# A two-layer graph kernel on one core: three products with both weight halves side by side, the first normalisation on ScalarE, and head and tail in orders of their own

## Chip, cores and metric

One Trainium2 chip, one of its cores. The metric is the device time in microseconds of one execution of the whole program; the data lie in HBM at the start and the result goes back there.

## What is computed

Eight graphs (B = 8) of N = 1024 nodes with D = 128 features, each with a dense 1024 x 1024 adjacency of zeros and ones. All data are float32.

```python
v, q, k = relu(x @ Wv + bv), relu(x @ Wq + bq), relu(x @ Wk + bk)
att = softmax(scores * adj - 9e15 * (1 - adj))        # scores = q @ k.T
x = layernorm(x + relu(att @ v @ Wo + bo))
h = x @ W_w.T + W_b
u = adj * exp(e[:, :, None] + f[:, None, :] + a_b)    # e = h @ a1, f = h @ a2
out = layernorm(x + (u / u.sum(axis=2, keepdims=True)) @ h)
```

## The kernel before

Nodes are taken in T = 8 tiles of 128. Nearly every matrix operand is split in two fp32r parts, a rounded one ("hi", here `h`) and what is left ("lo", here `l`), and a product of two matrices is three matmuls (hi x hi, lo x hi, hi x lo) that are summed in PSUM (`product`, L824 to L826). So each operand costs a rounding, mostly on ScalarE (ACT), and a subtraction, on VectorE (DVE, out of PSUM) or GpSimd (POOL, in SBUF).

For one batch: `project_q` and `project_k` make q and k transposed, in halves of 512 nodes; `project_v` makes v in halves of four tiles. ACT evicts q and k with bias and relu, DVE evicts v (`v_out`, L568). For each of 8 tiles `scores` fills the two banks of `s_ps`; DVE adds the penalty of the absent edges and finds the row extreme (`mask_max`, L578); ACT takes the exponential (`probs`); PE transposes it in two halves (`transpose_p`, into `pt_ps`), ACT and DVE split it (`prob_hi`, `prob_lo`). `attend` multiplies two tiles with v at a time (into `av_ps`), again split by `av_hi` and `av_lo`. `project_out` multiplies with Wo, in two halves; DVE scales by the row sum and adds the bias in place in PSUM (`o_out`, L596 to L601), adds x (`residual0`, L608), takes statistics (`stats0`), POOL the power -1/2, DVE normalises (`norm0`, L630). For the second layer `transpose_x1`, `x1_hi`, `x1_lo`, then `project_h` (130 columns: h and the two logit parts), `exp_ef`, and g = h times an exponential, split out of PSUM by `g_hi` (ACT, L446) and `g_lo` (DVE, L642). `aggregate` multiplies a tile of the rounded transposed adjacency (`round_adj`, ACT, L370, from two staging slots into a ring of four) with all of g, 8 matmuls of 258 columns; DVE adds the two parts (`agg_out`, L655). Then the row scale (`scale_out`), the residual (`residual1`, POOL), statistics, power and second normalisation (`norm1`, POOL) and the store. POOL also turns each adjacency tile into a penalty (`convert`, L256) and makes the lower parts of x, q, k and v.

Order: every engine, and SP with its queue of transfers, has one list of steps written by hand (`batch_pass`), run for all passes with the parts of absent batches left out; three batches are in flight. What PE puts in PSUM outside the scores, transposes and `attend` goes round three banks `m_ps` in the order of the table `SLOTS`, 22 uses a pass; PE waits in `shared` until the use three places before has been evicted. `transpose_p` waits for `prob_lo` of the tile before, `scores` for `mask_max` of the tile before, `k_hi` of a batch for the last scores of the batch before. The head is the same list with most parts absent: x first, q before k, lower parts on POOL. The tail is the same list too: the last batch's eight aggregations come after all the rest, each behind its `round_adj`, and then `scale_out`, `residual1` in halves, `stats1`, the power, `norm1` and two stores.

Of the kernel before, what the change touches and what calls it, by code (L numbers as in the profile page):

```python
# [5 lines left out]
F32 = mybir.dt.float32  # L6
# [6 lines left out]
EPS = 1e-5  # L13
# [4 lines left out]
def resnorm_kernel(nc, x, x_t, adj, adj_t_tiles, pack_a, pack_b, out):  # L18
# [11 lines left out]
    WARM = 13  # L30
    assert D == P and T == 8

    with ExitStack() as ctx:
# [13 lines left out]
        w_h, w_l = sb("w_h", [P, 4, D], F32R), sb("w_l", [P, 4, D], F32R)  # L47
# [26 lines left out]
        ef = sb("ef", [P, T, 2])  # L74
        g = sb("g", [P, T, 2, G1], F32R)
# [8 lines left out]
        var0, var1, rstd0, rstd1 = (sb(n, [P, T]) for n in ("var0", "var1", "rstd0", "rstd1"))  # L84
# [34 lines left out]
        out_free = [sem(f"out_free{k}") for k in range(2)]  # L119
        passed = sem("passed")  # L120
# [38 lines left out]
        SLOTS = (  # L159
# [4 lines left out]
        )  # L164
        PASSES = range(-1, B + 2)
        filled, bank, before = [], {}, {}
        for p in PASSES:
            for what, part, behind in SLOTS:
                if there(p - behind):
                    use = (what, p - behind, part)  # L170
                    bank[use] = m_ps[len(filled) % BANKS]
                    before[use] = filled[-BANKS] if len(filled) >= BANKS else None
                    filled.append(use)

        emptied = {"q": (q_evac, 2), "k": (k_evac, 2), "v": (v_evac, 2), "o": (y_done, 2), "x1t": (x1tl_done, 2),
                   "h": (gl_done, TH), "agg": (agg_done, T)}
# [5 lines left out]
        def _(sp):  # L182
# [900 lines left out]
```

## Time and profile before

| | us |
|---|---|
| runs (3): lowest, median, highest | 435.87, 435.93, 440.18 |
| the profiled execution, whole | 435.52 |
| its span in the trace | 433.8 |
| PE busy | 405.0 |
| DVE busy | 325.8 |
| ACT busy | 307.1 |
| POOL busy | 260.9 |

The span reaches from the first to the last recorded event; what lies around it, 1.7 us, is start and end of the program. The granted clock of PE has a mean of 0.976 of full speed. The engines: PE is TensorE (PEld its loading of weights), DVE is VectorE, ACT ScalarE, POOL GpSimd, SP the engine that issues transfers. L and a number is a line of the kernel. Busy intervals of PE overlap the next one's start, so the distance from one start to the next tells what a matmul takes in a sequence.

### The profile page before, as it was taken

The page shows a single profiled execution, that of the slowest core. Times are in us where ns is not written, and L with a number is a line of the kernel's source. Part 1 is how long each engine was busy: PE and PEld are TensorE (multiplying, and loading weights), DVE is VectorE, ACT ScalarE, POOL GpSimd, SP SyncE. Part 2 cuts the span into 40 slices and gives each one's busy share as a digit, 9 for nine tenths or more (in the row PEclk, how much of TensorE's full clock was granted, in tenths as well). Part 3 has the DMA queues.
Part 4 walks back from the last instruction along what each step waited for, and adds up shares of the span by engine and source line. Part 5 has one row for each costly group of instructions (what it writes and reads, how often), then busy time and mean ns, then how long its engine had stood idle before and what let it go on. Part 6 is the DMA issues. An engine that isn't in the chain of part 4 may idle for free.

```text
span 433.8 us, 8721 instructions
## 1 busy us (share of the span) xinstructions
PE 405.0 (93%) x2944; PEld 377.6 (87%) x2944; DVE 325.8 (75%) x929; ACT 307.1 (71%) x569; POOL 260.9 (60%) x223
## 2 busy tenths in 40 slices
PE   8699999999999999999999999999999999997730
PEld 7589999999999999999999999999999999996630
DVE  2566689587887888797887878787887979878631
ACT  4586779787878778696878778696878677765510
POOL 3943753474266972779356972779357852752955
PEclk9999999999999999999999999999999999999685
DMA  6763355465472739385474738385464737247431
GB/s 225 247 249 100 97 195 210 179 202 187 163 275 85 261 113 335 97 278 194 153 286 115 275 107 328 108 280 201 138 251 107 269 116 254 81 146 219 171 97 48
DMA packets 36684, 80.72 MB, mean 186 GB/s; under 512 B 2592, under 2 KB 19104, under 8 KB 36640
## 3 DMA queue, kind: packets, MB, share of 16 engines
q1 hardware_dynamic: 36352, 79.70, 54.4%
q8 instruction: 24, 0.39, 0.3%
q10 hardware_dynamic: 288, 0.46, 0.3%
q14 instruction: 20, 0.16, 0.1%
HBM read 75.96 MB, written 4.19 MB: 185 GB/s over the span
## 4 chain that ended last, share of the span: by engine, by line
PE 85%; POOL 5%; DVE 4%; DMA 3%; ACT 2%; issue 1%; POOLq 0%; DVEq 0%; ACTq 0%
PE pt_ps L877 12%; PE m_ps L928 12%; PE av_ps L889 7%; PE av_ps L890 7%; PE av_ps L891 7%; PE s_ps L824 7%; PE s_ps L826 7%; PE s_ps L825 6%; PE m_ps L826 6%; PE m_ps L825 6%; PE m_ps L824 6%; DMA adjt_in<-in_adj_t_dram 2%; PE m_ps L906 2%; DMA xt_in<-in_x_t_dram 1%; DVE prob L578 1%
## 5 line engine op out<-in xcount | busy, mean ns | idle before, releaser
L586 DVE TENSOR_TENSOR prob_tl<-pt_ps,prob_th 128x512 fp32r<-128x512 f32 x128 | 84.5, 682 | 24.5 <-ACT prob_th L417 24.4
L578 DVE CUSTOM_DVE_ANT_0 prob<-s_ps,penalty 128x1024 f32<-128x1024 f32 x64 | 78.0, 1219 | 23.4 <-PE s_ps L826 21.5
L417 ACT ACTIVATE prob_th<-pt_ps 128x512 fp32r<-128x512 f32 x128 | 73.1, 593 | 28.4 <-PE pt_ps L877 28.3
L370 ACT ACTIVATE adj_t<-adjt_in 128x1024 fp32r<-128x1024 f32 x64 | 67.1, 1056 | 24.7 <-PE m_ps L928 13.8
L409 ACT ACTIVATE prob<-prob,neg_max 128x1024 f32<-128x1024 f32 x64 | 73.8, 1152 | 12.5 <-DVE neg_max L578 12.4
L928 PE MATMUL m_ps<-g,adj_t 128*128 128x258 f32 x512 | 76.2, 295 | 4.9 <-DVE g L649 1.9
L877 PE MATMUL pt_ps<-ident,prob 128*128 128x128 f32 x512 | 73.7, 273 | 0.0
L889 PE MATMUL av_ps<-prob_th,vh 128*128 128x256 f32 x256 | 73.6, 287 | 0.0
L928 PEld LDWEIGHTS m_ps<-g,adj_t 128*128 128x128 f32 x512 | 67.2, 195 | 6.4 <-ACT adj_t L370 2.7
L891 PE MATMUL av_ps<-prob_th,vl 128*128 128x256 f32 x256 | 72.4, 283 | 0.0
L890 PE MATMUL av_ps<-prob_tl,vh 128*128 128x256 f32 x256 | 72.3, 283 | 0.0
L256 POOL TENSOR_SCALAR penalty<-adj_in 128x1024 bf16<-128x1024 f32 x64 | 66.4, 1051 | 5.9 <-issue 5.9
L877 PEld LDWEIGHTS pt_ps<-ident,prob 128*128 128x128 f32 x512 | 59.2, 140 | 5.4
L824 PE MATMUL s_ps<-kh,qh 128*128 128x512 f32 x128 | 53.2, 416 | 3.8 <-DVE neg_max L578 2.2
L265 POOL TENSOR_TENSOR ql<-qf,qh 128x512 fp32r<-128x512 f32 x16 | 20.6, 1286 | 55.7 <-ACT qh L388 55.6
L826 PE MATMUL s_ps<-kh,ql 128*128 128x512 f32 x128 | 50.3, 393 | 0.0
L825 PE MATMUL s_ps<-kl,qh 128*128 128x512 f32 x128 | 50.2, 392 | 0.0
L889 PEld LDWEIGHTS av_ps<-prob_th,vh 128*128 128x128 f32 x256 | 49.0, 191 | 0.3 <-issue 0.2
L890 PEld LDWEIGHTS av_ps<-prob_tl,vh 128*128 128x128 f32 x256 | 49.0, 191 | 0.1
L891 PEld LDWEIGHTS av_ps<-prob_th,vl 128*128 128x128 f32 x256 | 49.0, 191 | 0.0
L655 DVE TENSOR_REDUCE gs<-m_ps 128x129 f32<-128x258 f32 x64 | 25.9, 419 | 19.0 <-POOL out_sb L303 10.0
L269 POOL TENSOR_TENSOR kl<-kf,kh 128x512 fp32r<-128x512 f32 x16 | 20.6, 1287 | 20.3 <-ACT kh L400 20.3
(101 smaller groups left out, 881.4 us busy)
## 6 DMA issues: line engine op xcount, KB each, us to landing
adj_in<-in_adj_dram SPq DMA_DIRECT2D x64, 512.0 KB, 4.3
adjt_in<-in_adj_t_dram SPq DMA_DIRECT2D x64, 512.0 KB, 4.3
xt_in<-in_x_t_dram SPq DMA_DIRECT2D x8, 512.0 KB, 6.6
x_in<-in_x_dram SPq DMA_DIRECT2D x8, 512.0 KB, 4.7
out_dram<-out_sb SPq DMA_DIRECT2D x16, 256.0 KB, 4.4
wb<-in_pack_b_dram ACTq DMA_DIRECT2D x1, 320.0 KB, 6.3
wa<-in_pack_a_dram ACTq DMA_DIRECT2D x1, 132.0 KB, 4.4
```

The lines of the kernel that those rows point to most:

```text
L409: sc.activation(prob[i % 2][:, :], prob[i % 2][:, :], ACT.Exp, bias=neg_max[:, i:i + 1], scale=-1.0, accum_out=row_sum[b % 2][:, i:i + 1]) ...
L417: sc.activation(prob_th[n % 2][:, tiles(k), (i % 2) * P:(i % 2 + 1) * P], pt_ps[k][:, :].rearrange("p (c n) -> p c n", n=P), ACT.Copy).the ...
L578: v.tensor_tensor_reduce(out=prob[i % 2][:, :], in0=s_ps[:, :, :].rearrange("p a n -> p (a n)"), in1=penalty[:, n % RING, :], scale=-1.0, ...
L586: v.tensor_tensor(prob_tl[n % 2][at], pt_ps[k][:, :].rearrange("p (c n) -> p c n", n=P), prob_th[n % 2][at].bitcast(F32), ALU.subtract).th ...
L824: pe.matmul(dst, lh, rh, start=True, stop=False)
L825: pe.matmul(dst, lh, rl, start=False, stop=False)
L826: return pe.matmul(dst, ll, rh, start=False, stop=True)
L877: last = pe.transpose(blk(pt_ps[k], c), blk(prob[i % 2], k * TH + c), ident[:, :])
L889: pe.matmul(av_ps[:, 0:PAIR], vh[:, c, :], th[:, c, :], start=(c == 0), stop=False)
L890: pe.matmul(av_ps[:, 0:PAIR], vh[:, c, :], tl[:, c, :], start=False, stop=False)
L891: last = pe.matmul(av_ps[:, 0:PAIR], vl[:, c, :], th[:, c, :], start=False, stop=(c == T - 1))
L928: last = pe.matmul(a[:, 0:2 * G1], adj_t[:, n % RING, c, :], g[:, c, :, :].rearrange("p a e -> p (a e)"), start=(c == 0), stop=(c == T - 1))
```

## The change

Three products, v, output projection and h, are now made with the high and low weight halves in one moving operand (`w_hl`, `w1hl`): the first matmul has 256 (260) columns and leaves hi x hi and hi x lo beside each other in PSUM, the second adds lo x hi to the first half. The eviction adds the two. v and the output projection now go through a bank two tiles at a time (four parts a batch), h one tile at a time (eight parts).

```diff
+            def product_side_by_side(dst, lhs, rhs, width):
+                lh, ll = lhs
+                pe.matmul(dst, lh, rhs, start=True, stop=False)
+                return pe.matmul(dst[:, 0:width], ll, rhs[:, 0:width], start=False, stop=True)
...
-            def v_out(b, k):
...
-                v.tensor_tensor(half(vf, k).rearrange("p (t d) -> p t d", d=D),
...
-                                rows(minus_bv[:, :], TH), ALU.max).then_inc(v_evac, 1)
+            def v_out(b, j):
...
+                v.tensor_reduce(vf[:, j * PAIR:(j + 1) * PAIR].rearrange("p (t d) -> p t d", d=D),
+                                halves(bank["v", b, j][:, :], D), AX_X, ALU.add).then_inc(v_evac, 1)
...
-                for c in range(TH):
-                    j = k * TH + c
-                    o = blk(bank["o", b, k], c)
-                    v.scalar_tensor_tensor(out=o, in0=o, scalar=inv_sum[:, j:j + 1], in1=bo_full[:, :],
+                v.tensor_reduce(o_sum[:, :, :], halves(bank["o", b, j][:, :], D), AX_X, ALU.add).then_inc(o_summed, 1)
...
+                for c in range(2):
+                    t = 2 * j + c
+                    v.scalar_tensor_tensor(out=o[:, c, 0, :], in0=o_sum[:, c, :], scalar=inv_sum[:, t:t + 1], in1=bo_full[:, :],
```

The bias of v, before folded into a maximum with -bv and into `bo_full` (a third product of `form_w1`, now gone, with `bo_full` now the plain row), is added by POOL, then the maximum with zero (`v_bias`). h is summed into SBUF by DVE (`h_out`); g is made there by ACT (`g_full`), rounded by ACT (`g_hi`, two of 512) and its lower part is taken by POOL. The first normalisation is `Identity` with scale and bias on ACT, and DVE makes the bias:

```diff
-            def norm0(b, k):
-                dve.wait_ge(rstd0_done, b + 1)
...
+            def shift_mean0(b, k=None):
...
+                v.scalar_tensor_tensor(out=shift0[:, at], in0=mv0[:, at, 0], scalar=-1.0, in1=rstd0[:, at],
+                                       op0=ALU.mult, op1=ALU.mult).then_inc(shift0_done, 1)
...
+                    sc.activation(x1[:, j, :], x1[:, j, :], ACT.Identity, bias=shift0[:, j:j + 1],
+                                  scale=rstd0[:, j:j + 1]).then_inc(x1_done, 1)
...
+            def v_bias(b, k):
...
+                gp.tensor_tensor(half(vf, k).rearrange("p (t d) -> p t d", d=D), half(vf, k).rearrange("p (t d) -> p t d", d=D),
+                                 rows(bv_row, TH), ALU.add).then_inc(v_biased, 1)
...
+                gp.tensor_scalar(half(vf, k), half(vf, k), 0.0, None, ALU.max).then_inc(v_relu, 1)
```

Every engine now has three lists: `head` (batch 0 up to its third `attend`, and batch 1's projections), `batch_pass` for the passes 1 to 6, and `tail`. The bank table has 30 uses a pass. In the head k comes before q, the transposed x is loaded in halves, the second pack of weights is loaded by SP behind it, and the lower parts of the first x, k and q are made by DVE; the warm-up on PE has 9 products in place of 13. In the tail the last batch's first six tiles of adj_t go into buffers that are free by then, its first five sums go into the banks of scores, transposes and `attend`, with the first half of g as soon as that is there, and its end runs in pairs of tiles: scale, residual and statistics on DVE, power on POOL, normalisation on ACT, four stores.

```diff
-    WARM = 13
+    EARLY = 5
+    WARM = 9
...
+            if i < 6:
+                return (qh, ql, kh, kl, xth, xtl)[i][:, :].rearrange("p (t d) -> p t d", d=P)
...
+        for i, ps in enumerate((s_ps[:, 0, :], s_ps[:, 1, :], pt_ps[0], pt_ps[1], av_ps)):
+            bank["agg", LAST, i] = ps
...
+            def residual1_pair(g_):
...
+                    v.scalar_tensor_tensor(out=gs[:, t, 0:D], in0=gs[:, t, 0:D], scalar=scale1[:, t:t + 1],
+                                           in1=x1b[:, t, :], op0=ALU.mult, op1=ALU.add).then_inc(r1_last, 1)
```

Of the changed kernel's order, the places that matter most. PE, the output projection in a pass behind half of k, before, the first of its four tiles (`w_h`, `w_l` are the weight halves, `avh`, `avl` the attention sum's; a row's size is what it writes):

```order
L824 MATMUL m_ps<-xth,w_h 128x512
L825 MATMUL m_ps<-xtl,w_h 128x512
L826 MATMUL m_ps<-xth,w_l 128x512
L824 MATMUL m_ps<-w_h,avh 128x128
L825 MATMUL m_ps<-w_l,avh 128x128
L826 MATMUL m_ps<-w_h,avl 128x128
```

and now, behind a v part, parts 1 and 2 of it:

```order
L1406 MATMUL pt_ps<-ident,prob 128x128 x4
L1354 MATMUL m_ps<-w_hl,xth 128x256
L1355 MATMUL m_ps<-w_hl,xtl 128x128
L1354 MATMUL m_ps<-w_hl,xth 128x256
L1355 MATMUL m_ps<-w_hl,xtl 128x128
L1406 MATMUL pt_ps<-ident,prob 128x128 x4
L1354 MATMUL m_ps<-w_hl,avh 128x256
L1355 MATMUL m_ps<-w_hl,avl 128x128
```

Three rows a tile have become two, the first twice as wide, and a part is two tiles. DVE, the eviction of an output half in a pass, before:

```order
L578 ISA neg_max 128x1
L586 TENSOR_TENSOR prob_tl<-pt_ps,prob_th 128x4x128 x2
L596 RECIPROCAL inv_sum<-row_sum 128x4
L601 SCALAR_TENSOR_TENSOR m_ps<-m_ps,inv_sum,bo_full 128x128 x4
L608 SCALAR_TENSOR_TENSOR x<-m_ps,x_in 128x512
L578 ISA prob,neg_max<-s_ps,penalty 128x1024
```

and now, part 1, with three more such places a pass (`wb` is the tensor that holds the bias row of the output):

```order
L932 RECIPROCAL inv_sum<-row_sum 128x2
L934 TENSOR_REDUCE o_sum<-m_ps 128x256
L939 SCALAR_TENSOR_TENSOR m_ps<-o_sum,inv_sum,wb 128x128 x2
L913 ISA prob,neg_max<-s_ps,penalty 128x1024
L913 ISA neg_max 128x1
L921 TENSOR_TENSOR prob_tl<-pt_ps,prob_th 128x4x128
L947 SCALAR_TENSOR_TENSOR x<-m_ps,x_in 128x256
```

A reduce into SBUF stands before each pair, and the pair's inputs are `o_sum` and the row of `wb`. PE at the end of the program, before the last batch's aggregations were one row (`L928 MATMUL m_ps<-g,adj_t 128x258 x64`) behind the products of h; now:

```order
L1483 MATMUL s_ps<-g,qh 128x258 x4
L1483 MATMUL s_ps<-g,ql 128x258 x4
L1483 MATMUL pt_ps<-g,kh 128x258 x4
L1483 MATMUL s_ps<-g,qh 128x258 x4
L1483 MATMUL s_ps<-g,ql 128x258 x4
L1483 MATMUL pt_ps<-g,kl 128x258 x4
L1483 MATMUL pt_ps<-g,kh 128x258 x4
L1483 MATMUL pt_ps<-g,kl 128x258 x4
L1483 MATMUL av_ps<-g,xth 128x258 x8
L1483 MATMUL m_ps<-g,xtl 128x258 x8
L1483 MATMUL m_ps<-g,adj_t 128x258 x16
```

The first three rows are half sums with the first half of g (a fourth and fifth follow further on), and `qh` to `xtl` hold adj_t.

## Rows read from the trace of the kernel before

**Rows 1.** Page, part 1: busy us (share of the span) and instructions of each engine.

```profile
PE 405.0 (93%) x2944; PEld 377.6 (87%) x2944; DVE 325.8 (75%) x929; ACT 307.1 (71%) x569; POOL 260.9 (60%) x223
```

**Rows 2.** Two stretches in the middle: busy us of each engine, clock, DMA share, GB/s.

```profile
165.00:214.00 49.00, 49.00 (x366) 46.12 (x365) 39.88 (x115) 38.05 (x72) 32.51 (x27) 1.00 0.60 203
214.00:263.00 49.00, 49.00 (x366) 46.08 (x365) 39.87 (x115) 37.80 (x72) 32.52 (x27) 1.00 0.60 205
```

**Rows 3.** Timeline of PE in one stretch: start us, us, then the matmul.

```profile
222.03 0.28 PE L824 MATMUL m_ps<-w_h,xth 128*128 128x128 f32 x1
222.37 0.28 PE L824 MATMUL m_ps<-w_h,xth 128*128 128x128 f32 x1
...
228.66 0.28 PE L891 MATMUL av_ps<-prob_th,vl 128*128 128x256 f32 x1
228.78 0.28 PE L889 MATMUL av_ps<-prob_th,vh 128*128 128x256 f32 x1
```

**Rows 4.** Groups by line: count | busy us, mean ns of one | idle before.

```profile
L655 DVE TENSOR_REDUCE gs<-m_ps 128x129 f32<-128x258 f32 x64 | 25.9, 419 | 19.0 <-POOL out_sb L303 10.0 <-PE m_ps L928 8.9
L568 DVE TENSOR_TENSOR vf<-m_ps,minus_bv 128x512 f32<-128x512 f32 x16 | 10.9, 680 | 1.2 <-PE m_ps L826 1.2
L601 DVE SCALAR_TENSOR_TENSOR m_ps<-m_ps,inv_sum,bo_full 128x128 f32<-128x128 f32 x64 | 18.2, 352 | 0.6
L446 ACT ACTIVATE g<-m_ps,ef 128x128 fp32r<-128x128 f32 x64 | 20.1, 367 | 1.2
L256 POOL TENSOR_SCALAR penalty<-adj_in 128x1024 bf16<-128x1024 f32 x64 | 66.4, 1051 | 5.9 <-issue 5.9
```

**Rows 5.** Single lines: ns min/median/max of one, first and last start.

```profile
L672 DVE TENSOR_SCALAR var<-mv x8: 163/650/1099, 142.5 to 424.7; 128x8 f32<-128x8 f32 x8
...
L625 DVE TENSOR_SCALAR var<-mv x8: 171/172/173, 67.7 to 394.2; 128x8 f32<-128x8 f32 x8
...
L642 DVE SCALAR_TENSOR_TENSOR g<-m_ps,ef,g x64: 317/344/354, 79.9 to 404.9; 128x128 fp32r<-128x128 f32 x64
```

**Rows 6.** Timeline of DVE and POOL in the set-up.

```profile
8.70 0.43 DVE L684 TENSOR_TENSOR w_l<-wb,w_h 128x256 fp32r<-128x256 f32 x1
...
17.73 3.10 POOL L256 TENSOR_SCALAR penalty<-adj_in 128x1024 bf16<-128x1024 f32 x3
...
19.07 0.86 DVE L706 TENSOR_TENSOR w1l<-w1f,w1h 128x130 fp32r<-128x130 f32 x1
```

**Rows 7.** Timeline of the head.

```profile
5.25 0.29 DVE L676 CAST w_h<-wa 128x256 fp32r<-128x256 f32 x1 [5.25 <-DMA wa<-in_pack_a_dram]
...
5.82 2.56 POOL L261 TENSOR_TENSOR xtl<-xt_in,xth 128x512 fp32r<-128x512 f32 x2 [4.41 <-ACT xth L376]
...
7.27 0.47 PE L824 MATMUL m_ps<-xth,w_h 128*128 128x512 f32 x1 [0.27 <-POOL xtl L261]
...
10.28 1.29 POOL L265 TENSOR_TENSOR ql<-qf,qh 128x512 fp32r<-128x512 f32 x1 [1.91 <-ACT qh L388]
...
13.00 1.27 POOL L269 TENSOR_TENSOR kl<-kf,kh 128x512 fp32r<-128x512 f32 x1 [0.18 <-ACT kh L400]
...
14.32 0.50 PE L824 MATMUL s_ps<-kh,qh 128*128 128x512 f32 x1 [1.48 <-POOL kl L269]
```

**Rows 8.** Timeline of the tail.

```profile
387.70 0.28 PE L891 MATMUL av_ps<-prob_th,vl 128*128 128x256 f32 x1
...
405.37 4.86 PE L928 MATMUL m_ps<-g,adj_t 128*128 128x258 f32 x24 [1.91 <-DVE g L649]
...
410.11 1.06 ACT L370 ACTIVATE adj_t<-adjt_in 128x1024 fp32r<-128x1024 f32 x1 [1.55 <-DMA adjt_in<-in_adj_t_dram]
...
415.06 1.06 ACT L370 ACTIVATE adj_t<-adjt_in 128x1024 fp32r<-128x1024 f32 x1 [2.15 <-DMA adjt_in<-in_adj_t_dram]
...
416.16 1.23 PE L928 MATMUL m_ps<-g,adj_t 128*128 128x258 f32 x8 [0.95 <-ACT adj_t L370]
...
424.96 1.65 POOL L298 TENSOR_TENSOR rstd<-var,minus_half 128x8 f32<-128x8 f32 x1 [1.72 <-DVE var L672]
...
429.99 1.04 POOL L306 TENSOR_TENSOR out_sb<-out_sb,rstd 128x512 f32<-128x512 f32 x1
```

**Rows 9.** Stretch of the tail, columns as in rows 2.

```profile
400.00:410.00 10.00, 7.84 (x46) 7.40 (x45) 6.48 (x29) 5.53 (x16) 8.95 (x7) 0.66 0.55 186
```

More of the change, by code:

```diff
@@ L156, in stand_alone @@
             eng.sem_inc(passed, 1)
-        SLOTS = (
[4 rows of a table removed]
-        )
-        PASSES = range(-1, B + 2)
-        filled, bank, before = [], {}, {}
-        for p in PASSES:
[L168 to L176, printed above, removed]
+        PASSES = range(1, B - 1)
@@ new lines, in resnorm_kernel @@
+        filled = list(HEAD_SLOTS)
+        for p in PASSES:
+            filled += [(what, p - behind, part) for what, behind, part in PASS_SLOTS if there(p - behind)]
+        filled += TAIL_SLOTS
+        bank = {use: m_ps[n % BANKS] for n, use in enumerate(filled)}
+        before = {use: filled[n - BANKS] if n >= BANKS else None for n, use in enumerate(filled)}
+        for i, ps in enumerate((s_ps[:, 0, :], s_ps[:, 1, :], pt_ps[0], pt_ps[1], av_ps)):
+            bank["agg", LAST, i] = ps
@@ L241, in _ @@
+            head()
+            for p in PASSES:
                 batch_pass(p)
+            tail()
             for k in range(2):
-                sp.wait_ge(out_free[k], 16 * B)
+                sp.wait_ge(out_free[k], 16 * LAST)
+            sp.wait_ge(stored_last, 16 * TH)
         @block.gpsimd
@@ L357, in _ @@
+            constants()
             head()
-            for p in range(-1, B + 3):
+            for p in PASSES:
                 batch_pass(p)
+            tail()
         @block.scalar
@@ L558, in _ @@
+            sc.dma_start(wa[:, :], pack_a).then_inc(wa_arrived, 16)
+            head()
+            for p in PASSES:
                 batch_pass(p)
+            tail()
         @block.vector
@@ L611, in stats @@
-            def stats(b, k, src, stat, mv, stat_done, mv_done):
-                for j in range(k * TH, (k + 1) * TH):
+                dve.wait_ge(o_scaled, T * b + 2 * j + 2)
+                o = bank["o", b, j][:, :].rearrange("p (t a d) -> p t a d", a=2, d=D)
+                v.scalar_tensor_tensor(out=x1[:, pair(j), :], in0=o[:, :, 0, :], scalar=0.0, in1=x_in[b % 2][:, pair(j), :],
+                                       op0=ALU.max, op1=ALU.add).then_inc(y_done, 1)
+            def stats(b, at, src, stat, mv, stat_done, mv_done):
+                for j in range(at.start, at.stop):
@@ L814, in _ @@
+            head()
+            for p in PASSES:
                 batch_pass(p)
-                if p == 0:
-                    split_w1()
+            tail()
         @block.tensor
@@ L1033, in batch_pass @@
-                if there(p):
-                    scores(p, 7)
-                    transpose_p(p, 5, 1)
+                project_k(p + 1, 0)
+                transpose_p(p, 3, 0)
+                project_v(p + 1, 1)
+                scores(p, 5)
+                transpose_x1(p - 1, 0)
+                transpose_p(p, 3, 1)
+                transpose_x1(p - 1, 1)
+                attend(p, 0)
+                project_h(p - 1, 0)
+                project_h(p - 1, 1)
+                project_h(p - 1, 2)
```

1533 lines of the change are left out of this document (1055 added, 478 removed), and 12 rows, old and new, of tables (HEAD_SLOTS, PASS_SLOTS, SLOTS).

## Prediction

> **What bounds the kernel now.** I read the page's busy shares first, then stretches of 49 us, then the waits, and last head and tail in order of time. The page gives PE 93% of the span, DVE 75%, ACT 71%, POOL 60% [rows 1]. A busy PE need not be a full one, so the stretches matter. From 67 us on the program repeats once per batch of the eight: two stretches of 49.0 us one behind the other hold the same numbers of instructions, PE is busy all 49.00 us of each, DVE 39.9, ACT 38, POOL 32.5 [rows 2]. By the starts inside such a stretch three 128-wide products take 0.34 us (0.112 each) and a 256-wide one 0.12 [rows 3]. All the products of a batch add up to 49 us at such paces, so PE is really full there and the others have 9 to 16 us to spare. In that loop only PE's work sets the time. Head and tail are different. The first scores start at 14.32 us behind four lower parts on POOL [rows 7]; after the last `attend`, which ends at 387.8 us, come 46.0 us in which PE waits often and the last 16.4 us have no matmul at all [rows 8].
>
> **The products.** v, output projection and h are 8 tiles each, three products a tile. Now each is two: one of 256 (260 for h) columns and one of 128 (130). By rows 3 a tile goes from 3 x 0.112 = 0.336 us to 0.12 + 0.112 = 0.232, which saves 0.104; 24 tiles a batch are 2.5 us, 192 tiles 20.0 us. All of it lies on PE's full stretch. Nothing else in PE's loop changes in amount, so PE needs 49.0 - 2.5 = 46.5 us a batch. The set-up loses one product pair: 0.2 us.
>
> **What the other engines get in exchange, per batch.** Prices are means [rows 4]. The reduce that adds the halves reads 512 numbers of PSUM; the one of L655 reads 258 in 0.42, the 512-wide DVE rows take 0.68, so 0.68. DVE loses v's eviction (2 x 0.68), two reciprocals (0.17 each, as the shortest DVE rows), the output's 8 x 0.35 and two residuals of v's width (0.68), and, at the same 0.35, eight normalisations and eight lower parts of g: 11.4 in all. It gains 4 + 4 reduces of 0.68, 4 reciprocals, the same 8 x 0.35, 4 residuals of 0.42, 8 h reduces of 0.42 and a shift of 0.17: 14.2. Net +2.7: DVE goes from 39.8 to 42.5 of 46.5. ACT gains 8 normalisations (by L446, 0.37), two roundings of g (0.63) and loses two exponentials (0.27): near 41. POOL gains v's bias (up to the 1.29 of a lower part [rows 7]) and maximum (0.5 to 1.05, half or all of L256) twice, and g's lower part (2 x 1.29): near 38.7. So everybody fits under 46.5, but DVE's reserve shrinks from 9.2 to 4.0 us.
>
> I also put PE's and DVE's new orders of one pass side by side, adding up these prices. The new pass turns the three shared banks 30 times instead of 22, and DVE arrives 0.8 to 3 us before PE needs a bank. The tightest place on another engine is the next batch's k: its rounding waits for all eight scores, and rounding 0.63, lower part 1.29, g's lower part 1.29 and lower part 1.29 follow on ACT and POOL (4.5 us, near 4.8 with hand-overs), under 5.4 us of PE work that stands between scores 7 and the next scores 0. It fits by half a microsecond.
>
> **The cost that no sum of durations shows.** Some DVE instructions of before are stretched. The set-up's `w1l`, both inputs in SBUF, is 130 wide and took 0.86 us, while the 256-wide one of the same kind took 0.43; it began at 19.07, POOL was inside a run of three converts of 1.03 us each, the second of which ends at 19.8, and `w1l` ended at 19.93 [rows 6]. The 8-wide `var` of the second normalisation takes 0.163 to 1.099 us, its twin of the first 0.171 to 0.173, when POOL is waiting for it [rows 5]. The 64 instructions of g's lower part (L642), with one tile in PSUM and one in SBUF, stay within 0.317 to 0.354 [rows 5]. So a DVE instruction of the first sort seems to stand until POOL's present one ends. The Trainium skill (SBUF — State Buffer, "Who interferes with whom") says that a VectorE instruction with two SBUF inputs contends with a GpSimd one that reads SBUF, and that the loser waits for the whole instruction. By that rule the new `o_out` would be hit, since the sum now lies in SBUF; the trace agrees for `w1l` (0.86 us), and no row of before shows the form in question. With the rule applied to both instructions of each pair the time is that of rival C; without it, that of A.
>
> In before `o_out` reads its number from PSUM. Now it reads `o_sum` and the bias row, both SBUF: 8 instructions a batch in 4 pairs. POOL will be busy 38.7 of 46.5 us, with pieces of mostly 1.05 to 1.3 us, so an instruction that comes at a random moment waits near 0.5. From below the cost is nothing (rows like L601's 0.35 hold). From above both of a pair wait, the first 0.5 and the second a whole POOL instruction of 1.1, because POOL's next one enters between them: 4 x 1.6 = 6.4 us. Four small ones (the shift, two of the row scale, g's column) now also meet a busy POOL: 0 to 2.0. I take the first of each pair and the small ones: 4 x 0.5 + 2.0 = 4.0 us. That makes DVE 46.5, as full as PE. Two engines that hand to each other in fixed orders are not both full; I allow 1.0 us a pass for that (0 to 3): a pace of 47.5. Six passes and a tail that behaves like one and a half: 7.5 us.
>
> **The head.** k comes first, x and its transfer are in halves, and the lower parts of x, k, q move from POOL to DVE. In before four of POOL's lower parts (near 1.28 each) stand in the chain to the first scores [rows 7]; the same width on DVE is 0.68. That is up to 2.4 us and perhaps 0.6 from the halved transfer. But these are two-SBUF instructions beside POOL's converts. Between -3 and +2, I take -1.5. The first product cannot come much before 7.27: the weights' land only at 5.25 and their split is 0.7 us [rows 7].
>
> **The tail.** Before, from the end of the last `attend`: 46.0 us. The chain to the last g takes 17.5; then eight aggregations of 0.96 need 12 us, since the rounding of adj_t waits for a free slot and a transfer (the rows at 410.11 and 415.06 waited 1.55 and 2.15) [rows 8]; then 16.4 us of row scale, residual, statistics, power, normalisation on POOL and the store. Now six more tiles of adj_t go into q, k and x buffers that are free by then, half the sum of five tiles runs before the second half of g, and the end goes in pairs over DVE, POOL, ACT. My count in the new order: last output projection and its eviction 3.8, statistics and power 3.3, normalisation, transposition and split 3.6, h, exp, g and its lower part 7.3 (POOL has a 1.65 power of batch 6 ahead of it): g at 18.0. Eight aggregations end near 24.3, the seventh and eighth still behind their transfers (two staging slots). DVE has 2.7 us per pair (two reduces 0.7, scale 0.55, residual 0.55, statistics 0.8, variance 0.1) from 18.6 on: 29.3. Then power 1.65, shift, normalisation 0.6, store 2.8 (the last piece of before ends at 431.0 of 433.8) [rows 8]: 34.8. PE does two and a half aggregations' worth more ahead of the last `attend`: +2.6. So 46.0 becomes 37.4; 1.1 of the 8.6 is product saving already counted, which leaves -7.5 (bounds -12 and 0). The clock stood at 0.66 between 400 and 410 us, behind waits of PE, between its levels of 1.2 and 2.4 GHz [rows 9]; similar waits remain, so I count no gain.
>
> **The sum.** Profiled span 433.8 - 20.0 - 0.2 - 1.5 - 7.5 + 7.5 = 412.1; the profiled execution took 435.52, which is 1.7 more, so 413.8. The runs' median is 435.93, 0.4 above the profiled one: I say 414.
>
> **Rivals.**
> A, no wait at the SBUF side for `o_out`. For it: the rows of L601 and L642 hold still, and nothing of before shows the new form. Then DVE is at 42.5 to 44 and PE stays full: 414 - 7.5 = 406.5.
> D, head and tail give nothing: the halves only feed a DVE that POOL holds up in the head, and in the tail the pair chain on DVE (10.7 us) takes what the earlier aggregation gave. For it: 29.3 against 24.3 in my own count. 414 + 1.5 + 7.5 = 423.
> C, slower: both of each `o_out` pair wait. DVE then needs 42.5 + 6.4 + 2.0 = 50.9 a pass, against 49.0 in all of before, and with 0.7 for hand-overs the loop runs at 51.6. Seven passes' worth of 51.6 - 46.5 are 35.7 over the time of A: 406.5 + 35.7 = 442. It decides from the point where a pass takes 50.7, that is 8.2 us of waits on DVE. Against it: POOL slackens as the pass grows, and DVE's starts overlap its predecessor by 0.08 us, so the second may be asked for before the first lets go.
>
> **How the numbers follow.** Forecast 0.36, A 0.30, D 0.16, C 0.18. The likeliest case by itself spans 409 to 421. A's lower edge is 400 (tail at -12, head at -3 with some cost left); half of C lies above 440. So 401 to 434 leaves out some 0.16 in C and 0.04 below. A measurement of this kernel tells about 1% (4.4 us) from no change. Faster by more than that is below 431.6: forecast, A, D and 0.01 of C, 0.83. Within: 0.08, the milder part of C. Slower: 0.09.
>
> **What would show it.** The loop's period, by one instruction's starts a batch apart: 46.5 for A, near 47.5 for me, over 50 for C. The mean of the new `o_out` instruction: 0.35 is A, 0.6 mine (one of two stretched by 0.5), 1.1 C; and whether a stretched one ends just after a POOL instruction. PE's products of 256 columns at 0.12 us apart; if they cost more, the 20 us are wrong. PE should have short waits for DVE in the loop where it had none. First scores near 12.8 us. After the last matmul 10 to 11 us. If PE waits for POOL's `kl` or for ACT instead, the chain through k was the tight one, and I have put the cost at the wrong place.

## The result and the profile after

The changed kernel took 446.26 us (median of 4 runs, 445.92 to 446.90); the kernel before, on the same chip, 438.06 (435.87 to 441.15). The ratio is 1.0184, 95% interval 1.0104 to 1.0264: slower, by 1 to 2.6%, where 414 was predicted. Three later sets of runs, beside the experiments below, put the kernel before at medians of 435.6 to 436.4. Its single runs gather at 435 to 437 and at 438 to 442 us, which makes most of the width of every interval here. The profiled execution took 446.42 us, its span is 444.7.

The page, part 1, of the kernel after:

```profile
PE 399.8 (90%) x2742; PEld 359.9 (81%) x2742; DVE 377.5 (85%) x983; ACT 337.9 (76%) x642; POOL 312.6 (70%) x262
```

Beside [rows 1] PE has 5.2 us less, DVE 51.7 more, POOL 51.7 more, ACT 30.8 more, and no engine is above 90%. Four periods of the loop of after, from one batch's first transposition of x1 to the next one's (columns as in [rows 2]):

```profile
123.30:173.20 49.90, 47.73 (x341) 43.51 (x341) 44.92 (x118) 41.44 (x80) 40.94 (x33) 1.00 0.55 192
173.20:224.60 51.40, 49.23 (x340) 44.85 (x340) 45.07 (x118) 41.38 (x80) 40.79 (x33) 0.97 0.61 203
224.60:275.40 50.80, 47.94 (x341) 43.54 (x341) 45.16 (x118) 41.51 (x80) 40.67 (x33) 1.00 0.56 187
275.40:325.30 49.90, 47.75 (x341) 43.54 (x341) 44.95 (x118) 41.34 (x80) 40.95 (x33) 1.00 0.59 203
```

A period is 50.5 us on average against 49.0 in [rows 2], PE is idle for 2.2 to 2.9 us of it, and DVE, at 45, isn't full either. Groups of after that answer to [rows 4], then one line's min/median/max:

```profile
L939 DVE SCALAR_TENSOR_TENSOR m_ps<-o_sum,inv_sum,wb 128x128 f32<-128x128 f32 x64 | 49.2, 813 | 3.8 <-DVE o_sum L934 0.5
L639 ACT ACTIVATE x<-x,shift,rstd 128x128 f32<-128x128 f32 x64 | 25.6, 483 | 2.2 <-DVE shift L970 2.2
L981 DVE TENSOR_REDUCE h_sb<-m_ps 128x130 f32<-128x260 f32 x64 | 24.7, 422 | 4.4 <-PE m_ps L1355 4.2
L398 POOL TENSOR_SCALAR vf<-vf 128x512 f32<-128x512 f32 x16 | 24.1, 1509 | 1.4
L395 POOL TENSOR_TENSOR vf<-vf,wb 128x512 f32<-128x512 f32 x16 | 20.6, 1289 | 0.0
L934 DVE TENSOR_REDUCE o_sum<-m_ps 128x256 f32<-128x512 f32 x32 | 21.4, 669 | 0.0
```

```profile
L939 DVE SCALAR_TENSOR_TENSOR m_ps<-o_sum,inv_sum,wb x64: 347/769/1525, 44.3 to 409.2; 128x128 f32<-128x128 f32 x64
```

The output's scaling has the same shape as L601 in [rows 4], and went from 352 to 813 ns; its shortest is still 347. That is 64 x 0.46 = 29.5 us on DVE in all, 3.7 a batch. Where they stand beside POOL (timeline of both engines, after, one batch):

```profile
240.75 1.29 POOL L389 TENSOR_TENSOR kl<-kf,kh 128x512 fp32r<-128x512 f32 x1 [5.19 <-ACT kh L611]
241.95 2.80 DVE L939 SCALAR_TENSOR_TENSOR m_ps<-o_sum,inv_sum,wb 128x128 f32<-128x128 f32 x2
242.00 1.29 POOL L431 TENSOR_TENSOR g<-h_sb,g 128x512 fp32r<-128x512 f32 x1
243.25 1.35 POOL L389 TENSOR_TENSOR kl<-kf,kh 128x512 fp32r<-128x512 f32 x1
...
249.89 1.49 POOL L398 TENSOR_SCALAR vf<-vf 128x512 f32<-128x512 f32 x1
250.99 0.62 DVE L939 SCALAR_TENSOR_TENSOR m_ps<-o_sum,inv_sum,wb 128x128 f32<-128x128 f32 x2
...
255.72 1.04 POOL L444 TENSOR_TENSOR out_sb<-out_sb,rstd 128x512 f32<-128x512 f32 x1
256.00 1.95 DVE L939 SCALAR_TENSOR_TENSOR m_ps<-o_sum,inv_sum,wb 128x128 f32<-128x128 f32 x2 [0.46 <-DVE o_sum L934]
```

The pair that starts at 241.95 takes 2.80 us and covers POOL's two instructions from 242.00 to 244.60; the one at 256.00 takes 1.95. Unhindered a pair takes 0.62, and that is also what the pair at 250.99 takes, beside POOL's maximum of v (the fourth of the batch, not shown, takes 0.63 beside the other maximum). So two of four pairs are held up, by 2.2 and 1.3 us, and the kind of POOL instruction matters. How long a pair stands also depends on where it lands: in three of the other loop batches the third pair starts just ahead of a POOL instruction, its first one takes 0.36, only the second is held, and the pair takes 1.40.

What PE waits for in four periods (waits, 123.3 to 325.3 us: total, times, longest):

```profile
PEld m_ps L1435 <- ACT x L639: 5.4, 9, 0.7
PE m_ps L1454 <- DVE x L947: 4.2, 4, 1.1
PE m_ps L1454 <- DVE gs L993: 2.1, 4, 0.5
PE m_ps L1435 <- ACT x L639: 1.8, 4, 0.4
```

L947 is the residual behind the output's scaling: an aggregation waits for its bank. In the second of the four periods, and in no other, such waits were followed by a fall of PE's clock. PE stood still for 1.05 us (to 207.99) and 0.52 us (to 210.13), and from 210.2 on the clock was granted at half, 1.2 GHz, for 3.4 us:

```profile
206.80:210.20 3.40, 1.83 (x15) 1.60 (x13) 3.26 (x13) 1.84 (x4) 3.40 (x4) 1.00 0.50 154
210.20:213.60 3.40, 3.40 (x12) 3.04 (x13) 3.29 (x8) 2.19 (x4) 3.31 (x3) 0.50 0.10 11
213.60:217.00 3.40, 3.40 (x25) 3.17 (x24) 2.19 (x8) 2.16 (x3) 2.78 (x3) 1.00 0.96 334
```

That period is the longest of the four. A second such stretch (397.9 to 401.4) lies ahead of the last `attend`; e1 and e6 (below) have neither. What the clock alone cost isn't settled: in e9 three of four periods have such a stretch and are at most 0.5 us longer than the one without.

To see where the 10.9 us between the two spans lie, I cut both at the first transposition of x1 of a batch and at the end of the last `attend` (starts read off PE's timelines; e6 is an experiment below):

| stretch | before | after | e6 |
|---|---|---|---|
| start to batch 0's x1 | 71.3 | 73.3 | 69.5 |
| to batch 1's | 48.0 | 50.0 | 47.8 |
| four more batches | 196.0 | 201.9 | 191.3 |
| to batch 6's | 47.8 | 47.9 | 45.7 |
| to the end of the last `attend` | 24.7 | 33.0 | 29.2 |
| to the end of the span | 46.0 | 38.5 | 38.4 |

The last stretch gained 7.5 us; of those ahead of it none gained, and one stayed level.

### The profile page after: what moved, and what is told of

It reads as the page before. It is cut to its first block, busy times and chain, and to the rows that moved or that the text cites. A ratio compares the mean times of both kernels' runs of the same rounds, so it can differ in the third digit from the quotient of the medians.

```text
span 444.7 us, 8668 instructions
## 1 busy us (share of the span) xinstructions
PE 399.8 (90%) x2742; PEld 359.9 (81%) x2742; DVE 377.5 (85%) x983; ACT 337.9 (76%) x642; POOL 312.6 (70%) x262
## 4 chain that ended last, share of the span: by engine, by line
PE 31%; DVE 26%; ACT 15%; POOL 13%; issue 11%; DMA 3%; DVEq 0%; SPq 0%; ACTq 0%; POOLq 0%
PE m_ps L1454 8%; DVE m_ps L939 5%; ACT x L639 5%; DVE prob L913 4%; DVE prob_tl L921 4%; PE pt_ps L1406 3%; POOL penalty L376 3%; POOL g L431 3%; ACT adj_t L578 2%; PE m_ps L1354 2%; ACT h_sb L659 2%; DMA adj_in<-in_adj_dram 2%; DVE stat L952 2%; PE av_ps L1418 2%; PE av_ps L1419 2%
## 5 line engine op out<-in xcount | busy, mean ns | idle before, releaser
L921 DVE TENSOR_TENSOR prob_tl<-pt_ps,prob_th 128x512 fp32r<-128x512 f32 x128 | 85.6, 680 | 5.4 <-ACT prob_th L628 5.4
L1406 PE MATMUL pt_ps<-ident,prob 128*128 128x128 f32 x512 | 76.2, 276 | 3.8 <-DVE prob_tl L921 3.6
L376 POOL TENSOR_SCALAR penalty<-adj_in 128x1024 bf16<-128x1024 f32 x64 | 67.5, 1060 | 12.9 <-DMA adj_in<-in_adj_dram 6.9
L1454 PE MATMUL m_ps<-g,adj_t 128*128 128x258 f32 x448 | 66.1, 294 | 11.1 <-DVE x L947 7.6
L1454 PEld LDWEIGHTS m_ps<-g,adj_t 128*128 128x128 f32 x448 | 60.0, 196 | 15.1 <-issue 7.6
L578 ACT ACTIVATE adj_t<-adjt_in 128x1024 fp32r<-128x1024 f32 x58 | 60.2, 1053 | 12.1 <-PE m_ps L1454 8.4
L1406 PEld LDWEIGHTS pt_ps<-ident,prob 128*128 128x128 f32 x512 | 58.1, 141 | 11.9 <-DVE prob_tl L921 6.4
L939 DVE SCALAR_TENSOR_TENSOR m_ps<-o_sum,inv_sum,wb 128x128 f32<-128x128 f32 x64 | 49.2, 813 | 3.8 <-DVE o_sum L934 0.5
L389 POOL TENSOR_TENSOR kl<-kf,kh 128x512 fp32r<-128x512 f32 x14 | 18.4, 1316 | 47.8 <-ACT kh L611 47.8
L1347 PEld LDWEIGHTS s_ps<-kh,qh 128*128 128x128 f32 x128 | 24.3, 190 | 8.0 <-DVE neg_max L913 2.3
```

Source lines behind the costliest of these rows:

```text
L376: gp.tensor_scalar(penalty[:, n % RING, :], adj_in[:, n % RING, :], PENALTY, -PENALTY, ALU.mult, ALU.add).then_inc(penalty_done, 1)
L921: v.tensor_tensor(prob_tl[n % 2][at], pt_ps[k][:, :].rearrange("p (c n) -> p c n", n=P), prob_th[n % 2][at].bitcast(F32), ALU.subtract).th ...
L939: v.scalar_tensor_tensor(out=o[:, c, 0, :], in0=o_sum[:, c, :], scalar=inv_sum[:, t:t + 1], in1=bo_full[:, :], op0=ALU.mult, op1=ALU.add). ...
L1347: pe.matmul(dst, lh, rh, start=True, stop=False)
L1406: last = pe.transpose(blk(pt_ps[k], c), blk(prob[i % 2], k * TH + c), ident[:, :])
L1454: last = pe.matmul(a[:, 0:2 * G1], adj_tile(b, i)[:, c, :], g[:, c, :, :].rearrange("p a e -> p (a e)"), start=(c == 0), stop=(c == T - 1))
```

## The experiments

Two theories stood at the start. P: DVE's instructions that read only SBUF wait for POOL's running one, this is what holds up the output's eviction, its bank and so PE. N: the cost is in the longer chains themselves (v's bias and maximum on POOL, the normalisation on ScalarE), and the stretched rows are a by-product.

**e1: the output's scaling reads PSUM and one SBUF tile.** In `o_out`, for each pair (lines shortened):

```
-v.tensor_reduce(o_sum[:, :, :], halves(bank[...], D), AX_X, ALU.add)
+v.scalar_tensor_tensor(out=o_sum[:, c, :], in0=o[:, c, 1, :], scalar=inv_sum, in1=bo_full, mult, add)    # c = 0, 1
...
-v.scalar_tensor_tensor(out=o[:, c, 0, :], in0=o_sum[:, c, :], scalar=inv_sum, in1=bo_full, mult, add)
+v.scalar_tensor_tensor(out=o[:, c, 0, :], in0=o[:, c, 0, :], scalar=inv_sum, in1=o_sum[:, c, :], mult, add)
```

> The changed kernel (446.3), with the output's eviction in another form: no reduce; two instructions a part scale and add the bias to the upper halves out of PSUM (PSUM and SBUF in, SBUF out), two more scale the lower halves in PSUM and add those. Same result, about the same DVE work by the rows (4 x 0.35 against 0.67 + 2 x 0.35), but never two SBUF inputs. Theory P (waits of two-SBUF instructions for POOL): the mean of the final instruction falls from 0.81 to 0.35, that is 29 us of DVE; the loop's period falls from 50.6 to 47 to 48 and the time to 418 to 430. Rival N (the normalisation on ACT, on which x1's transposition waits, sets the period): 440 or more. Rival M (POOL is too full because of the maximum of v, 1.51 us each): 438 or more.

Measured 430.42 us (429.50 to 430.77), ratio to before 0.9852 (0.9806 to 0.9898), at the edge of what theory P gave and clear of both rivals. The scaling is back at 354 ns, and a period at 49.0, where 47 to 48 were expected:

```profile
169.19:218.12 48.93, 47.48 (x340) 43.52 (x340) 41.96 (x122) 41.52 (x80) 40.48 (x33) 1.00 0.58 201
```

So 16 us of the time went with the form of this eviction. But the period is only that of before, not the 46.5 that the products should leave.

**e2: no maximum of v; e3: e2 with e1's eviction.** Both leave out the clipping of v at zero (v goes on unclipped), which takes L398 off POOL:

```
-gp.tensor_scalar(half(vf, k), half(vf, k), 0.0, None, ALU.max).then_inc(v_relu, 1)
```

> The changed kernel without the maximum with zero on v (v is left unclipped: 16 instructions of 1.51 us on POOL fall away, the rest is as it was). Theory P: POOL is not the bound; fewer POOL instructions hit fewer of the pairs, -2 to -6 us: 440 to 444. Rival M: POOL's 24 us are on the path: 425 to 435. Rival N: no change, 445 to 447.

> e1's eviction and v left unclipped as in e2. Theory P: within 4 us of e1, since without the waits POOL has time to spare. Rival M: well below both, under 415. If e1 alone gave little and this gives much, both causes cover each other.

e2 took 449.55 us (ratio 1.0302, 1.0229 to 1.0375), 3.3 more than after, which no theory had foretold: the scaling's mean rose to 868 ns. The second pair of each loop batch, which takes 0.62 beside the maximum, now meets the second layer's normalisation on POOL and takes 2.12 (at 250.39 us in e2). e3 took 424.34 (0.9716, 0.9671 to 0.9761), 6.1 less than e1, between what P and M had said, with a period of 47.85. The same 3 us of POOL a batch are worth 6 in one kernel and nothing in the other.

**e4: the normalisation back on DVE, rest as after** (eight `tensor_scalar` of 128x128 at the shift's place, none on ScalarE).

> The changed kernel with the first normalisation back on DVE, at the place where DVE makes the shift; ACT loses 64 x 0.48 = 31 us, DVE gets 64 x 0.34. Theory P: DVE is the engine that lacks time, so this costs: 446 to 456. Rival N: the wait for ACT before x1's transposition goes (the trace shows 14 us of such waits on PE and its weight loads): 430 to 440.

456.1 us, ratio 1.0444 (1.0393 to 1.0495), 10 more than after. Taking the normalisation off ScalarE doesn't bring the time back. It isn't a clean test of ScalarE's part, because the new DVE instructions read and write SBUF alone and are held up by POOL too: the eight of batch 0 take 6.32 us, and in each of the five loop batches one of the eight takes 1.3.

**e6: e1 with the maximum of v done on ScalarE.** This computes what the kernel computes:

```
-pool.wait_ge(v_biased, 2 * b + k + 1)
-gp.tensor_scalar(half(vf, k), half(vf, k), 0.0, None, ALU.max).then_inc(v_relu, 1)
...
+act.wait_ge(v_biased, 2 * b + k + 1)
+sc.activation(half(vf, k), half(vf, k), ACT.Relu).then_inc(v_relu, 1)
```

> The one-input eviction of e1 with the maximum of v taken over by ScalarE (a Relu in place in two halves, then the rounding), GpSimd keeps only the bias: GpSimd 40.5 - 3.0 = 37.5 us a pass as in e3, ScalarE 41.5 + 2 x 0.63 = 42.8 of 49.0, and v's path is 0.9 us shorter per half than in e1 but 0.6 longer than in e3 (424.3). Theory, that GpSimd's long maximum held up 1.15 us of each pass in e1 (430.4): 424 to 428. Rival, that ScalarE's order (normalisation ahead of the x1 transposition) sets e1's pace of 49.0, so that 1.3 us more in front of it costs: 431 to 438.

424.68 us (424.29 to 425.39), ratio 0.9732 (0.9681 to 0.9783), within 0.4 of e3. It beats both kernels: 2.7% under before. Its loop (a period) and its waits of PE over four periods:

```profile
166.68:214.51 47.83, 47.25 (x340) 43.49 (x341) 41.86 (x122) 42.45 (x82) 37.47 (x31) 1.00 0.61 212
```

```profile
PEld m_ps L1437 <- ACT x L638: 4.8, 8, 0.7
PE m_ps L1437 <- ACT x L638: 1.8, 4, 0.4
PEld m_ps L1349 <- issue: 1.0, 4, 0.2
```

PE is busy 47.25 of 47.83, and its only wait for another engine is the one for the normalisation, 0.45 a batch (that of its weight loads, 1.2 a batch, runs beside its work).

**e8: the kernel before plus eight tiny DVE instructions a batch** at the place of the output's eviction, 128x8, both inputs in SBUF, four behind each half:

```
+for c in range(TH):
+    v.scalar_tensor_tensor(out=junk[:, k * TH + c, :], in0=bo_full[:, 0:8], scalar=inv_sum[:, k * TH + c:k * TH + c + 1],
+                           in1=wb_row[:, 0:8], op0=ALU.mult, op1=ALU.add).then_inc(junk_done, 1)
```

> The kernel before plus 8 VectorE instructions a batch of 128x8 elements with two inputs in SBUF, at the place of the output projection's eviction (four behind each half), into a tile nobody reads. Each does 0.17 us of work; if it waits for GpSimd's running instruction it is 0.5 to 0.9 long. VectorE: 39.9 + 8 x 0.17 = 41.3 a pass of 49.0 without the waits, 44 to 47 with them. Theory, that the kernel before has room for this on VectorE because TensorE was full: 436 to 442. Rival, that the delay is passed on even there since VectorE's results are due within a microsecond or two: 443 to 450.

447.81 us (444.46 to 447.94), ratio 1.0243 (1.0186 to 1.0299): the expectation fell. A period of e8, and the tiny group:

```profile
175.43:225.57 50.14, 49.21 (x365) 46.13 (x364) 41.45 (x123) 38.05 (x72) 32.49 (x28) 1.00 0.59 199
```

```profile
L607 DVE SCALAR_TENSOR_TENSOR junk<-bo_full,inv_sum,wb_row x64: 214/221/1317, 48.9 to 401.2; 128x8 f32<-128x8 f32 x64
```

DVE got 1.6 us more a batch and was 9 us short of full, yet the period rose by 1.1 to 1.5. POOL was idle beside one of the two groups of four (192.26 us, 0.63 for four), so only the other met a wait: its last instruction, 1.31 in each loop batch. PE's waits over four periods (122.05 to 322.99 us):

```profile
PE m_ps L934 <- DVE x L614: 3.8, 4, 1.0
```

L614 is the residual behind `o_out`, which PE didn't wait for in before. DVE's reserve is not free at this place: what stands behind `o_out` is a bank that PE needs soon.

**e9, e12, e13: e1 plus the tiny pairs, in three forms.** A pair behind each eviction of the output (lines shortened). e12 differs from e9 only in the first input; e13 has a single input tile:

```
+v.scalar_tensor_tensor(out=junk[...], in0=bo_full[:, 0:8], scalar=inv_sum[...], in1=wb_row[:, 0:8], mult, add)   # e9
+v.scalar_tensor_tensor(out=junk[...], in0=o[:, c, 1, 0:8], scalar=inv_sum[...], in1=wb_row[:, 0:8], mult, add)   # e12
+v.tensor_scalar(junk[...], bo_full[:, 0:8], inv_sum[...], None, mult)                                            # e13
```

> e1 plus the same 8 tiny instructions a batch with two inputs in SBUF, a pair behind each eviction of the output projection: the wait alone comes back, with 8 x 0.17 = 1.4 us of work a pass. Theory, that the waits behind GpSimd are what made the changed kernel 16 us slower than e1: each pair lasts 1.2 to 1.9 us on average, VectorE goes from 42.0 to 46 or 47 a pass, time 444 to 455. Rival, that the time went with the detour of the sum through SBUF and not with the waits: VectorE 43.5, time 431 to 437.

> e9 (e1 plus eight 128x8 instructions a batch) with the first input of each tiny instruction read from PSUM in place of SBUF: the same instruction, work and place, and no second SBUF input. Theory, that what e9 lost was the wait for GpSimd: each tiny instruction 0.2 us (minimum of e9: 0.213) and never over 0.3, VectorE 42.0 + 1.7 = 43.7 a pass, 430.4 + 0 to 8 = 431 to 438. Rival, that any extra instruction at that place costs this much: 448 to 454.

> e9 with each tiny instruction a TENSOR_SCALAR from SBUF to SBUF, with one input (128x8, multiplied by the same column). The kernel before has such instructions with a spread of 163/650/1099 ns, and others with none. Theory a, that one SBUF input and an SBUF output suffice for the wait: mean 0.6 to 0.8 us, time 448 to 456 as e9. Theory b, that only a second SBUF input waits: mean 0.16 to 0.2 us, time 431 to 438.

The tiny line of e9, e12 and e13 in turn, one fence each:

```profile
L948 DVE SCALAR_TENSOR_TENSOR junk<-wb,inv_sum,wb_row x64: 213/816/1334, 45.7 to 420.0; 128x8 f32<-128x8 f32 x64
```

```profile
L948 DVE SCALAR_TENSOR_TENSOR junk<-m_ps,inv_sum,wb_row x64: 214/218/219, 46.5 to 398.1; 128x8 f32<-128x8 f32 x64
```

```profile
L948 DVE TENSOR_SCALAR junk<-wb,inv_sum x64: 218/825/1351, 48.7 to 420.3; 128x8 f32<-128x8 f32 x64
```

e9 took 454.05 us (1.0419, 1.0347 to 1.0491), e12 433.43 (0.9906, 0.9867 to 0.9945), e13 454.81 (1.0382, 1.0292 to 1.0473). With one input in PSUM none of the 64 is over 0.219 us and the whole costs 3 us; with everything in SBUF, one input or two, the median is 0.82 and the cost 24. A pair of e9 beside POOL:

```profile
247.97 1.29 POOL L433 TENSOR_TENSOR g<-h_sb,g 128x512 fp32r<-128x512 f32 x1
248.53 2.01 DVE L948 SCALAR_TENSOR_TENSOR junk<-wb,inv_sum,wb_row 128x8 f32<-128x8 f32 x2
249.22 1.29 POOL L391 TENSOR_TENSOR kl<-kf,kh 128x512 fp32r<-128x512 f32 x1
```

Two instructions of 0.2 us last until 250.54, that is to the end of POOL's second one (250.51). The first waits for the rest of the running instruction, POOL's next enters, and the second waits for all of it. Theory P holds, and so does its hard form, that both of a pair wait, wherever the first lands inside a POOL instruction and another follows at once. DVE came to 48.6 us a batch in e9, more than the 46 or 47 expected, so e9 holds more waiting than after, which fits a cost of 24 and not 16.

**e10: e6 with narrow products.** Each side-by-side tile in three 128-wide instructions:

```
-pe.matmul(dst, lh, rhs, start=True, stop=False)
+pe.matmul(dst[:, 0:width], lh, rhs[:, 0:width], start=True, stop=False)
+pe.matmul(dst[:, width:2 * width], lh, rhs[:, width:2 * width], start=False, stop=False)
```

> e6 (one-input eviction, maximum of v on ScalarE, pace 47.83, 424.7 us) with each side-by-side tile issued as three 128-wide instructions in place of a 256-wide and a 128-wide one; arithmetic and evictions as in e6. TensorE has 24 x 0.104 = 2.5 us more a pass. Theory, that e6's pass is TensorE's own work (47.25 busy of 47.83): pace 50.1 to 50.4, 424.7 + 8 x 2.4 = 442 to 446, so that the wide products earn their 20 us in full once the port waits are gone. Rival, that hand-overs between engines set the pass and hide part of it: 425 to 436.

438.55 us (ten runs, 435.74 to 439.90), ratio 1.0033 (0.9993 to 1.0072): 13.9 more than e6, between the theory and its rival. The profiled execution is the fastest of the ten, and its span is 11.9 longer than e6's. The same change to e1 (e7) has no result. A period:

```profile
171.71:221.35 49.64, 49.19 (x365) 45.90 (x365) 43.80 (x122) 42.49 (x82) 37.49 (x32) 1.00 0.60 202
```

By starts, the 24 tiles take 8.05 us here and 5.84 in e6, 0.092 less a tile; the period differs by 1.8. So the wide products earned 12 to 14 us of the 20 predicted, and at most that, since a part of e10's time may lie elsewhere: DVE's 1.9 us more with the same instructions are two small SBUF-only ones (the shift 1.20 in place of 0.16, g's column 0.97 in place of 0.16), which in e10's timing happen to meet POOL.

**e11: e6 with the normalisation on DVE.**

> e6 with the first normalisation back on VectorE (8 instructions of 0.31 to 0.34 us in place of the small shift), ScalarE 42.45 - 3.2 = 39.3 a pass, VectorE 41.9 + 2.5 = 44.4 of 47.8. Theory, that in this kernel VectorE's backlog is what TensorE meets, while ScalarE has 5 us to spare: 426 to 434. Rival, that the normalisation on ScalarE stands on the way to the x1 transposition (TensorE waits 0.5 to 1.2 us there each pass), so that it costs what it saves: 421 to 425.5.

434.32 us, ratio 0.9935 (0.9891 to 0.9978), 9.6 more than e6 and just above the theory's range. A period rises by only 0.5 (48.3). Of the 10.3 us between the two spans 6.8 lie ahead of batch 1's x1 (start to batch 0's 71.5, to the next 52.6, in the places of the table). There the eight normalisations of batch 0, SBUF to SBUF, take 6.32 us together. In batch 6, with POOL idle, eight take 2.15; in each loop batch eight take 3.1 to 3.3, because one of them is held up for 1.0 to 1.1 us by the lower part of x:

```profile
168.81 3.10 DVE L966 TENSOR_SCALAR x<-x,mv,rstd 128x128 f32<-128x128 f32 x8
168.93 1.37 POOL L381 TENSOR_TENSOR xtl<-xt_in,xth 128x512 fp32r<-128x512 f32 x1
```

```profile
L966 DVE TENSOR_SCALAR x<-x,mv,rstd x64: 333/338/1470, 66.9 to 401.4; 128x128 f32<-128x128 f32 x64
```

## Why the prediction was wrong

- **Where the gap lies.** The span is 32.6 us over the forecast. The six passes hold 17.0 of it (8.0 more than before, where 15 less for the products and 6 more for waits had been foretold), head and tail the other 15.5 (2.8 more than before, where the terms of the prediction come to 12.7 less).
- **The loop.** "I allow 1.0 us a pass for that (0 to 3): a pace of 47.5" is the step that failed. The sum compared DVE's total with the period, as if a delay cost something only once the engine is full. The period was 50.5 with DVE, at 45.0, 5.5 us short of full: 4.0 us over the 46.5, beyond the bound of 3. e8 shows this apart from the change: 1.6 us more on a DVE with 9 us to spare cost 1.1 to 1.5. e12, with 1.0 more and no wait, costs 0.2. Steps from one period to the next, all measured: PE's own work 47.25 (e6), its remaining hand-overs 0.6 (e6), the maximum on POOL and not on ScalarE 1.15 (e1 against e6), the waits for POOL 1.5 (after against e1).
- **Which wait it would be.** "4 x 0.5 + 2.0 = 4.0 us" looks right beside the 8 x 0.46 = 3.7 that the trace has for `o_out` alone, but by luck: both terms were wrong. `o_out` waited 3.7 and not 2.0, and the four small ones 0.1 and not 2.0 (in the loop of after the shift takes 0.24, the others 0.16 or 0.17). DVE's work without waits was 41.5 where 42.5 was summed. The choice "I take the first of each pair" was wrong as mechanism: the second of a pair waits as well, often for a whole instruction (2.80 and 1.95 us above, 2.01 in e9), and sometimes it alone does. The mean of 0.81 us fell between my 0.6 and C's 1.1, because two pairs of four stand beside POOL's maximum, which hardly blocks. The argument against rival C, that the second may be asked for before the first lets go, is refuted. The rule of the Trainium skill (SBUF — State Buffer, "Who interferes with whom"), that the loser waits for the other's whole instruction, agrees with the trace where the other is a TENSOR_TENSOR or the conversion (0.35 to 0.81 us on average). It doesn't hold so for the maximum: that one reads SBUF, and a pair of two-input instructions beside it took its unhindered 0.62. The same section says that `tensor_scalar`, with one source, can enter a mode that contends with GpSimd as well; e13 agrees (0.82 us median), and I had not weighed that.
- **Rival C.** It gave 442 at a pace of 51.6 with 8.4 us of waits a batch, and was to decide from a pace of 50.7 on. The place and the mechanism were right. The pace was 50.5 with 3.7 us of waits, so the count of waits was too high, and 2.5 of the 4.0 us over 46.5 came from elsewhere (the steps above). That the time was 446 and so over C's is due to the head and the stretch to the last `attend`, not to C's own terms.
- **Rival D** (head and tail give nothing, 423) came true as well: together they lost 2.8 us against before. Neither the forecast nor C had counted with it.
- **Rival A** (406.5 without the waits) is e1: 430.4. Taking the waits away gives back 16 us, not the 40 by which after and A differ.
- **Products.** Predicted 0.104 us a tile and 20 us. By starts 0.092 (e10 against e6), 17.7 us, and 12 to 14 reached the time. Right in kind: the price per tile was 13% too high, and the time kept two thirds to four fifths of what the tiles gave. The split inside a tile was wrong, and the two errors nearly cancel: by starts the wide product takes 0.17 to 0.18 us and not 0.12, the narrow one behind it 0.06 to 0.08 and not 0.112. PE is busy 47.25 a batch in e6 and not 46.5: 0.3 of that is the price, the rest lies mostly at the transpositions of probabilities (6.89 us a batch by starts, 5.92 in before).
- **Other prices.** POOL's maximum 1.51 us against "0.5 to 1.05", since the row taken as its like is 128x1024 from f32 to bf16 and this one writes f32; ScalarE's normalisation 0.48 against 0.37; the reduces 0.67, 0.68 and 0.42, as said. POOL reached 40.5 to 41.3 a batch instead of 38.7, and having the maximum there and not on ScalarE cost 5.7 us of time (e1 against e6).
- **Head.** Predicted -1.5 (-3 to +2). The first product starts at 6.00 us (7.27 in [rows 7], and I had said it could not come much earlier), the first scores at 11.86, against 12.8 foretold. Yet batch 0's x1 comes 2.0 us later than before, and 1.8 earlier in e6. So the head's order looks good for what was said, with waits like those of the loop against it (the first two `o_out` pairs take 2.19 and 2.02).
- **Tail.** The working gave 34.8 us from the end of the last `attend`, and +2.6 ahead of it, which make the 37.4. Measured were 38.5, a gain of 7.5 where 11.2 was counted. g was ready after 18.6 (18.0 said), the last aggregation after 26.9 (24.3 said: PE's clock is granted at 0.57 and 0.69 in the last two rows below, and four matmuls take 0.86 to 0.99 us by starts in place of half of 0.96). And "PE does two and a half aggregations' worth more ahead of the last `attend`: +2.6" was 4.5 in e6 and 8.3 in after: the second step that failed. So the tail as a whole gave 3.1 us in e6 and nothing in after. The orders of head and tail were not tried by themselves; this is read from traces alone.

Stretches of the tail of after, to hold against [rows 9]; the column behind POOL's is the clock:

```profile
410.00:420.00 10.00, 6.18 (x33) 5.25 (x32) 7.85 (x35) 8.42 (x17) 5.87 (x6) 0.75 0.80 238
420.00:430.00 10.00, 7.96 (x40) 7.72 (x41) 3.75 (x17) 6.40 (x12) 8.69 (x8) 0.57 0.62 191
430.00:444.70 14.70, 3.10 (x26) 2.89 (x24) 9.45 (x47) 3.72 (x9) 4.47 (x6) 0.69 0.19 55
```

PE matmuls there, first half sums:

```profile
420.91 1.20 PE L1483 MATMUL s_ps<-g,qh 128*128 128x258 f32 x4 [1.07 <-issue]
421.90 1.06 PE L1483 MATMUL s_ps<-g,ql 128*128 128x258 f32 x4
422.76 1.06 PE L1483 MATMUL pt_ps<-g,kh 128*128 128x258 f32 x4
```

What stays open: why e6's PE spends that 1 us a batch more at its transpositions (the trace names no wait there), and how much of the head's and tail's result is due to their own orders.

## What to carry to other kernels

Before a sum is moved from a PSUM read to an SBUF tile, list the VectorE instructions that then touch SBUF alone, and what GpSimd runs beside them: here that one change cost 16 us, and reading one operand from PSUM (two short instructions in place of a reduce and a scaling) took it back. A reserve of busy time says little about an engine that hands over in a fixed order: test it by adding a known small dose at the place in question (e8, e12) before adding up totals. Work on GpSimd is worth what the instructions beside it make of it, so take it off only after the waits are gone (e2 against e3).

## What the runs showed of the hardware

- A VectorE instruction with all its operands in SBUF waited for GpSimd's running instruction even when it had one input and 8 columns (median 0.82 us against 0.22 with a PSUM input, same place and work). Larger one-input instructions wait as well: of e11's normalisations, 128x128 in place, one of eight took 1.3 to 1.5 us in each loop batch beside a lower part of POOL, where the others take 0.34.
- Two such instructions in a row can alternate with GpSimd: the first waits for the rest of the running instruction (0.75 in e9's pair), the second for the whole of the next (1.33). Where the first starts just ahead of a GpSimd instruction, only the second waits (0.36 and 1.14 at 154.36 us in after).
- GpSimd's in-place maximum on f32 (128x512, 1.49 us) hardly held VectorE up: five of the eight pairs beside it in the loop took 0.62 or 0.63, and the three that had begun before it 0.97 to 1.07. Its TENSOR_TENSOR forms and the conversion to bf16 did (in e9 a tiny pair beside two of those takes 1.87).
- The same small instruction took 0.16 us in e6 and 1.20 in e10, and the difference in the traces is when it came: 0.1 us after the start of a GpSimd instruction in e10, in the last 0.15 us of one in e6. A duration of an SBUF-only instruction read in one kernel is not its price in the next.
- Two idle times of TensorE, 1.05 us to 207.99 and 0.52 us to 210.13, were followed by 3.4 us at a granted clock of 0.50 (after, from 210.2 us); eight aggregation products took 1.98 us there, against 1.21 just before.
